# Expert stages of a four-layer attention and mixture-of-experts kernel: loops written out tile by tile, load order and the last bias changed

## What is computed

```
layer 0: 8 experts, best 2 a row, SwiGLU with 352 hidden units, and a shared expert
layer 1: 8 experts, best 1 a row, silu(x W1 + b1) W2 + b2 with 1,024 hidden units
layer 2: twice 32 experts, best 2 a row, SwiGLU with 128 hidden units, the two results averaged
layer 3: 32 experts, best 1 a row, SwiGLU, a fixed capacity of 80 rows an expert
y[row] = sum over the chosen experts e of weight(row, e) * expert_e(xn[row])
```

## Time and profile before

| | |
|---|---|
| runs | 2778.6 us in the median of three (2777.9 to 2780.2) |
| the profiled execution's own time | 2782.8 us |
| its span, first to last instruction | 2781.0 us |
| TensorE, products | busy 2143.0 us, 77% of the span |
| TensorE, weight loads | 1770.9 us, 64% |
| VectorE | 1327.0 us, 48% |
| ScalarE | 800.3 us, 29% |
| GpSimd | 790.9 us, 28% |
| mean granted TensorE clock | 0.868 of full speed |
| mean DMA rate | 124 GB/s over the span |

### The profile page before, as it was taken

The page is one execution under the profiler, slowest core; times in us unless marked ns, Lnnn a source line. Parts: engine busy times, 40 slices in busy tenths (PEclk is TensorE's granted clock), DMA queues, the critical chain, the costliest instruction groups (busy, mean ns, idle before and its releaser), DMA issues. The chain is left out here.

```text
span 2781.0 us, 46883 instructions
## 1 busy us (share of the span) xinstructions
PE 2143.0 (77%) x14782; PEld 1770.9 (64%) x14782; DVE 1327.0 (48%) x3863; ACT 800.3 (29%) x1862; POOL 790.9 (28%) x1177
## 2 busy tenths in 40 slices
PE   6769889955999999985996599847705773687695
PEld 5656659945999899975885366546604662354584
DVE  3555422235788788853002577452235225575513
ACT  4603312222333333342233144512201222244211
POOL 1000012232444444430112122024452434231133
PEclk9869999977999999996998699759856995898687
DMA  2030019933111111005883344038823873442195
GB/s 72 23 110 8 0 61 363 319 99 89 39 39 39 40 39 35 19 7 193 297 302 131 110 135 127 13 118 267 238 72 106 271 227 95 118 120 57 60 317 174
DMA packets 158190, 344.26 MB, mean 124 GB/s; under 512 B 22608, under 2 KB 101968, under 8 KB 149712
## 3 DMA queue, kind: packets, MB, share of 16 engines
q1 hardware_dynamic: 141136, 296.08, 32.5%
q0 software_dynamic: 16896, 46.16, 6.3%
HBM read 282.52 MB, written 57.15 MB: 122 GB/s over the span
## 5 line engine op out<-in xcount | busy, mean ns | idle before, releaser
L1821 PEld LDWEIGHTS heads_ps_c<-heads_band,heads_sT 128*128 128x128 f32 x3072 | 362.0, 192 | 21.3 <-issue 17.4
L1821 PE MATMUL heads_ps_c<-heads_band,heads_sT 128*128 128x129 f32 x3072 | 367.4, 276 | 7.4 <-DVE heads_band L2039 7.2
L930 DVE COPY experts_y<-experts_ps_y 128x256 f32<-128x256 f32 (+1 forms) x224 | 94.9, 424 | 503.2 <-DMA y_rows<-experts_y 288.1
L1977 POOL TENSOR_SCALAR heads_band<-heads_shifts,heads_taps 128x130 f32<-128x130 f32 x384 | 253.7, 675 | 268.2 <-PE heads_ps_c L1821 264.5
L853 PE MATMUL experts_ps_y<-experts_w,experts_h 128*128 128x256 f32 (+2 forms) x1008 | 269.7, 396 | 73.9 <-DVE experts_h L922 73.8
L843 PE MATMUL experts_ps_g<-experts_xT,experts_w 128*128 128x128 f32 (+2 forms) x2016 | 278.4, 286 | 6.5 <-ACT experts_xT L885 4.4
L843 PEld LDWEIGHTS experts_ps_g<-experts_xT,experts_w 128*128 128x128 f32 (+1 forms) x2016 | 258.1, 199 | 17.7 <-ACT experts_xT L885 12.2
L822 POOL DMA_INDIRECT experts_xg<-xn_rows,experts_x_ix x224 | 219.0, 978 | 176.4 <-POOL experts_x_ix L818 156.7
L818 POOL COPY experts_x_ix<-token_of 128x1 uint32 x224 | 41.5, 185 | 736.5 <-PEq L828 438.2
L853 PEld LDWEIGHTS experts_ps_y<-experts_w,experts_h 128*128 128x128 f32 (+2 forms) x1008 | 171.9, 189 | 113.2 <-DVE experts_h L922 93.7
L2039 DVE SCALAR_TENSOR_TENSOR heads_band<-heads_shifts,heads_taps,heads_band 128x130 f32<-128x130 f32 x768 | 226.3, 350 | 32.0 <-POOL heads_band L1977 27.5
(11 more groups left out here) (366 smaller groups left out, 3609.5 us busy)
## 6 DMA issues: line engine op xcount, KB each, us to landing
experts_w<-in_experts_dram SPq DMA_DIRECT2D x24, 2180.0 KB, 9.4
experts_w<-in_experts_dram SPq DMA_DIRECT2D x128, 384.0 KB, 4.6
experts_w<-in_experts_dram SPq DMA_DIRECT2D x40, 1088.0 KB, 8.6
y_rows<-experts_y SPq DMA_DIRECT2D x192, 128.0 KB, 8.9
experts_w<-in_experts_dram SPq DMA_DIRECT2D x32, 768.0 KB, 7.0
piece_rows<-heads_pieces SPq DMA_DIRECT2D x96, 192.0 KB, 2.6
heads_stackQ<-piece_rows SPq DMA_DIRECT2D x48, 192.0 KB
heads_stackK<-piece_rows SPq DMA_DIRECT2D x48, 192.0 KB
```

The costliest lines, as they stand in the source:

```text
L930: v.tensor_copy(y[0:rows, u % 2, :], ps_y[0:rows, u % 2, 0:D]).then_inc(y_copied, 1)
L1821: last = pe.matmul(out[:, qc * SEQ + k0:qc * SEQ + k1], sT[:, h % 2, kc, qc * P + dq:qc * P + dq + P], band[:, h % 2, dq, w0:w0 + k1 - k0] ...
L1977: last = pool.tensor_scalar(band[:, h % 2, dq, :], shifts[:, 0, :], taps[:, r % 2, h, dq * TAPS:dq * TAPS + 1], None, ALU.mult)
```

## The change

1. In `experts_stage` every engine's loop over blocks is written out over all tiles, so that the stagger of TensorE's three parts runs through the whole stage. All addresses are constants.
2. GpSimd hands column j of `token_of` to the gather directly, without the copy, and waits on `turned` (the transposition of tile j - ahead) rather than `y_ready`.
3. SyncE's load j waits on `y_copied` (the copy of tile j - ahead) rather than `y_ready`. The order of its queue stays: load j, store j - ahead.
4. NT is one less in layer 0 (39) and layer 1 (23), which still suffices: 8 experts can't leave more than 7 tiles over.
5. In experts1 the product with b2 goes; b2 is stored in all 128 rows of the weights, and VectorE adds it in the pass that took the output out of PSUM.
6. Waits that were made by giving semaphores a start value are made with `if j >= 2`.

```diff
 def experts_stage(...)
-        x_ix = s.sb("x_ix", [P, ahead, 1], U32)
-        b2 = lambda p: w[0:1, p, down_at + NF * D + NF:down_at + NF * D + NF + D]
+        b2 = lambda p: w[0:rows, p, down_at + NF * D + NF:down_at + NF * D + NF + D]
...
         def _(pool):
-            with pool.Fori(0, NT // ahead) as i:
-                for u in range(ahead):
-                    j = ahead * i + u
-
-                    pool.wait_ge(y_ready, j + 1)
-                    pool.tensor_copy(x_ix[:, u, :], tb.token_of[:, bass.ds(j, 1)]).then_inc(ix_ready, 1)
-                    pool.wait_ge(ix_ready, j + 1)
-
-                    pool.sem_inc(ix_passed, 1)
-                    pool.indirect_dma_start(xg[:, u, :], None, xn_dram,
-                                            bass.IndirectOffsetOnAxis(ap=x_ix[:, u, :], axis=0))\
-                        .then_inc(x_in[u], 16)
+            for j in range(NT):
+                if j >= ahead:
+                    pool.wait_ge(turned, j - ahead + 1)
+                pool.indirect_dma_start(xg[:, j % ahead, :], None, xn_dram,
+                                        bass.IndirectOffsetOnAxis(ap=tb.token_of[:, j:j + 1], axis=0))\
+                    .then_inc(x_in[j % ahead], 16)
...
         def _(pe):
-            def turn_rows(i, u):
-                pe.wait_ge(x_in[u], 16 * (i + 1))
+            def turn_rows(j):
+                pe.wait_ge(x_in[j % ahead], 16 * (j // ahead + 1))
+                if j >= 2:
+                    pe.wait_ge(xT_ready, j - 1)
...
+            def hidden_layer(j):
+                pe.wait_ge(xT_ready, j + 1)
+                pe.wait_ge(w_in[u], 16 * (j // ahead + 1))
+                if j >= 2:
+                    pe.wait_ge(h_ready, j - 1)
...
-                if biased:
-                    last = pe.matmul(ps_y[0:rows, p, 0:D], ones[0:1, 0:rows], b2(u), start=False, stop=True)
...
-            with pe.Fori(0, NT // ahead) as i:
-                for step in range(ahead + 2):
-                    for lag, part in enumerate((turn_rows, hidden_layer, output_layer)):
-                        if 0 <= step - lag < ahead:
-                            part(i, step - lag)
+            for step in range(NT + 2):
+                for lag, part in enumerate((turn_rows, hidden_layer, output_layer)):
+                    if 0 <= step - lag < NT:
+                        part(step - lag)
...
         def _(act):
-            with act.Fori(0, NT // ahead) as i:
-                for step in range(ahead + 1):
+            for step in range(NT + 1):
+                if step < NT:
+                    copy_rows(step)
+                if step >= 1:
+                    nonlinear(step - 1)
...
         def _(v):
-            def copy_out(i, u):
-                v.wait_ge(y_ready, ahead * i + u + 1 + ahead)
-
-                v.wait_ge(stored[u % 2], 16 * (ahead // 2 * i + u // 2 + 1))
-                v.tensor_copy(y[0:rows, u % 2, :], ps_y[0:rows, u % 2, 0:D]).then_inc(y_copied, 1)
+            def copy_out(j):
+                p = j % 2
+                v.wait_ge(y_ready, j + 1)
+                if j >= 2:
+                    v.wait_ge(stored[p], 16 * (j // 2))
+                if biased:
+                    v.tensor_tensor(y[0:rows, p, :], ps_y[0:rows, p, 0:D], b2(j % ahead), ALU.add)\
+                        .then_inc(y_copied, 1)
+                else:
+                    v.tensor_copy(y[0:rows, p, :], ps_y[0:rows, p, 0:D]).then_inc(y_copied, 1)
...
         def _(sp):
-            def load_weights(i, u):
-                j = ahead * i + u
-
-                sp.wait_ge(y_ready, j + 1)
-
-                sp.sem_inc(w_passed, 1)
-                row = sp.value_load(tb.weights_of[0:1, bass.ds(j, 1)], min_val=0, max_val=w_dram.shape[0] - P)
-                sp.dma_start(w[:, u, :], w_dram[bass.ds(row, P), :]).then_inc(w_in[u], 16)
+            def load_weights(j):
+                u = j % ahead
+                if j >= ahead:
+                    sp.wait_ge(y_copied, j - ahead + 1)
+                row = sp.value_load(tb.weights_of[0:1, j:j + 1], min_val=0, max_val=w_dram.shape[0] - P)
+                sp.dma_start(w[:, u, :], w_dram[bass.ds(row, P), :]).then_inc(w_in[u], 16)
+
+            def store(j):
+                sp.wait_ge(y_copied, j + 1)
+                sp.dma_start(y_dram[j * rows:(j + 1) * rows, :], y[0:rows, j % 2, :]).then_inc(stored[j % 2], 16)
+
+            for j in range(NT + ahead):
+                if j < NT:
+                    load_weights(j)
+                if j >= ahead:
+                    store(j - ahead)
...
 def build(...)
-        NT = TILES * 2 + 8
+        NT = TILES * 2 + 7
...
-        NT = TILES + 8
+        NT = TILES + 7
```

More of the change, by code:

```diff
@@ L842, in hidden_layer @@
                         for c in range(DC):
[L843 removed]
+                            last = pe.matmul(ps[0:m, p, f * P:f * P + rows], wt[:, c, f * P:f * P + m],
                                              xT[:, p, c, 0:rows], start=(c == 0), stop=(c == DC - 1))
                 last.then_inc(gu_ready, 1)
[L847 to L857 removed]
@@ L859, in _, with output_layer @@
-            with pe.Fori(0, NT // ahead) as i:
-                for step in range(ahead + 2):
-                    for lag, part in enumerate((turn_rows, hidden_layer, output_layer)):
-                        if 0 <= step - lag < ahead:
-                            part(i, step - lag)
+            def output_layer(j):
+                p, u = j % 2, j % ahead
+                pe.wait_ge(h_ready, j + 1)
+                if j >= 2:
+                    pe.wait_ge(y_copied, j - 1)
+                for f, m in enumerate(chunks):
+                    last = pe.matmul(ps_y[0:rows, p, 0:D], h[0:m, p, f, :], down_w(u)[0:m, f, :],
+                                     start=(f == 0), stop=(f == NF - 1))
+                last.then_inc(y_ready, 1)
@@ L924, in multiply @@
                 last.then_inc(h_ready, 1)
-            def copy_out(i, u):
-                v.wait_ge(y_ready, ahead * i + u + 1 + ahead)
-                v.wait_ge(stored[u % 2], 16 * (ahead // 2 * i + u // 2 + 1))
-                v.tensor_copy(y[0:rows, u % 2, :], ps_y[0:rows, u % 2, 0:D]).then_inc(y_copied, 1)
-            with v.Fori(0, NT // ahead) as i:
-                for step in range(ahead + 1):
-                    if step < ahead and not biased:
-                        multiply(i, step)
-                    if step >= 1:
-                        copy_out(i, step - 1)
+            def copy_out(j):
+                p = j % 2
+                v.wait_ge(y_ready, j + 1)
+                if j >= 2:
+                    v.wait_ge(stored[p], 16 * (j // 2))
+                if biased:
+                    v.tensor_tensor(y[0:rows, p, :], ps_y[0:rows, p, 0:D], b2(j % ahead), ALU.add)\
+                        .then_inc(y_copied, 1)
+                else:
+                    v.tensor_copy(y[0:rows, p, :], ps_y[0:rows, p, 0:D]).then_inc(y_copied, 1)
@@ L939, in _ @@
+            for step in range(NT + 1):
+                if step < NT and not biased:
+                    multiply(step)
+                if step >= 1:
+                    copy_out(step - 1)
         @block.sync
         def _(sp):
-            for p in range(2):
-                sp.sem_inc(stored[p], 16)
-            def load_weights(i, u):
-                j = ahead * i + u
-                sp.wait_ge(y_ready, j + 1)
-                sp.sem_inc(w_passed, 1)
-                row = sp.value_load(tb.weights_of[0:1, bass.ds(j, 1)], min_val=0, max_val=w_dram.shape[0] - P)
-                sp.dma_start(w[:, u, :], w_dram[bass.ds(row, P), :]).then_inc(w_in[u], 16)
@@ L953, in store @@
-            def store(i, u):
-                j = ahead * i + u
-                sp.wait_ge(y_copied, j + 3)
-                sp.dma_start(y_dram[dyn(j, rows), :], y[0:rows, u % 2, :]).then_inc(stored[u % 2], 16)
-            for u in range(ahead):
-                load_weights(0, u)
-            with sp.Fori(1, NT // ahead) as i:
-                for u in range(ahead):
-                    load_weights(i, u)
-                    store(i - 1, u)
-            for u in range(ahead):
-                store(NT // ahead - 1, u)
```

59 lines of the change are left out of this document (20 added, 39 removed).

## The result

The changed kernel took **2793.7 us** in the median of 16 runs against 2780.6 us for the kernel before in the same comparison: a ratio of 1.0048, 95% interval 1.0035 to 1.0060, so 13 us slower, and the whole interval lies on the slow side. The forecast was 2789, slower.

The account below looks back on a forecast made before the run. Experts2 and experts3 were taken as paced by a two-tile loop of copy, store and landing. Terms -1 (experts0), -28 (experts1), +28 (experts2), +12 (experts3) gave +11 us on 2782.8, so 2789 in the median, range 2757 to 2824.

Parts of the forecast that it names:

- rival 1: The forecast itself: the store loop, lengthened by the load in front, outweighs experts1's gain; 2785 to 2815 us, chance 0.45.
- SyncE's offsets: In experts2 the load leaves 1.23 us and the store 1.64 us after the start of the copy.
- The pace of experts2: 2.85 us a tile for 2.586 and 2.525, costing 12.7 and 15.6 us in the two experts2 stages.
- the shift of the twelve block starts: Twelve eight-tile block starts in experts2, each shifted to a load at 1.23 us, gave a mean of 2.85 us a tile.
- Rival 2: Queue empties, loads land in shortest times: 2.44 us a tile in experts2, sum -43, about 2736 us; chance 0.22.
- The start of experts2: Directly read index columns take 3.3 us off each stage (bounds 0 and 4.68), cancelling 3.3 us added for the backlog.
- Experts0: Pace of 4.45 us a tile, one tile less included: -1 us (-6 at 4.18, +14 at 5.1).
- Experts3: Pace of 3.7 us a tile for 3.172, over 22 tiles: +12 us.
- Experts1: Bias on VectorE, no gather wait or drain, one tile less: step of 7.4 us, stage -28 us.
- Rival 3: The two halves cancel to within 5.6 us, needing a pace near 2.73 us; chance 0.20.
- Rival 4: Queue stays as full as now: 3.09 us a tile in experts2, 4.19 in experts3, +50, so 2829 us; chance 0.07.
- Rival 5: The loops' 26 back jumps each cost an instruction fetch of 1.0 us; ending them gives 2763 us; chance 0.06.

Follow-up runs that it names:

- u_gather_old: Changed kernel with the gathers as before: index column copied by GpSimd, a wait for that copy, release by y_ready instead of turned; 2816.4 us, ratio 1.0094.
- u_y4: Changed kernel with four y buffers in SBUF rather than two, nothing else; 2672.1 us, ratio 0.9614.
- u_bias_pe: Changed kernel with the last bias of experts1 back on TensorE (product of ones with b2), plain copy on VectorE; 2824.9 us, ratio 1.0130.
- u_nt_old: Changed kernel with 40 tiles again in layer 0 and 24 in layer 1; 2805.7 us, ratio 1.0079.
- b_y4: Kernel before the change, loops kept, with four y buffers instead of two, nothing else; 2744.0 us, ratio 0.9837.
- u_load_early: Changed kernel with weight loads waiting on y_ready again, not on the copy, in every expert stage but experts1; 2723.2 us, ratio 0.9791.
- u_y8: Changed kernel with eight y buffers, order of load and store as changed; 2657.7 us, ratio 0.9558.

## Why the prediction was right, and where it was not

Sign, size and range held, by the mechanism of rival 1: the load in front of the store lengthens the loop over two tiles. That the sum came within 2 us is luck: experts0 was missed by 11 us, and experts1 and the two experts2 stages together by 4.5 and 6.5 the other way.

*SyncE's offsets.* Forecast 1.23 and 1.64 us after the copy, measured 1.19 and 1.57.

*The pace of experts2.* Forecast 2.85 us, measured 2.76 and 2.77. The step that failed is the shift of the twelve block starts: they were taken just after a backlog of stores, and the new loop has none; that this is why they came out too long was not tested. Nor were all twelve what the text says: in three of them the load had left 0.12, 0.42 and 1.10 us before the copy. By the form itself, half of 1.57 + 3.93 (from the issue of the store to the next copy but one, mean) is 2.75; the 3.93 are 3.84 of landing and 0.09 until VectorE starts. The waits of VectorE for stores grew by 41.7 us over both stages, from 83.2 and 83.7 to 104.7 and 103.9, for the 30 forecast. Rival 2 wanted landings of 3.2 us; with a quieter queue, a DMA share of 0.82, the median is 3.7 and 3.8, and single loads get down to 3.1. Its own turning point was a landing of 3.7, a pace of 2.68. The median is there, but the mean is 3.84, and the pace goes by the mean. The Trainium skill ("DMA: Bandwidth & Descriptors", section Anatomy of one DMA) fits a DMA that GpSimd issues with about 2.0 us plus bytes / 436 GB/s, an estimated 3.2 us for the 512 KB of load and store together. These DMAs are SyncE's, and the medians here are 0.5 us and more above that.

*The start of experts2.* I had set a loss of 3.3 us by the drained backlog against a gain of 3.3 by earlier gathers. The second turn waited 3.79 us after 4.68:

```profile
1841.85 0.69 PE L824 MATMUL experts_ps_x<-ident,experts_xg 128*128 128x128 f32 x2 [3.79 <-DMA experts_xg<-xn_rows,token_of]
```

From the first gather to the ninth copy the stages take 37.0 and 34.9 us where they took 35.1 and 33.2, so +1.9 and +1.8, and u_gather_old puts the share of the index copies and the release at -0.2 and +1.4 us. The lower bound, 0, was nearer than the upper. What cancels this is the tail: from copy 56 to the last 1.1 and 0.6 us less. The middle gives 48 x (2.757 - 2.586) = +8.2 and 48 x (2.766 - 2.525) = +11.6.

*Experts0* is the term I mis-sized most: -1 for +10.0. Two parts of it. The pace: I took 4.45, between 4.18 and 5.1, in the belief that an emptier queue would shorten the landing; it hardly did. The loads take 8.0 us (5.4 to 9.2) where they took 8.5, and the copies come in unequal pairs:

```profile
532.46 0.42 DVE L923 COPY experts_y<-experts_ps_y 128x256 f32<-128x256 f32 x1 [6.28 <-DMA y_rows<-experts_y]
535.68 0.42 DVE L923 COPY experts_y<-experts_ps_y 128x256 f32<-128x256 f32 x1 [2.27 <-DMA y_rows<-experts_y]
543.08 0.42 DVE L923 COPY experts_y<-experts_ps_y 128x256 f32<-128x256 f32 x1 [6.45 <-DMA y_rows<-experts_y]
```

That is 10.62 us for two tiles here, 2 x 4.77 in the mean. 23 tiles at 4.77 instead of 4.45 are +7.4 us. And the start, which I had not priced: from the first gather to the ninth copy 60.5 us for 52.4, so +8.0; the third copy came 14.0 us after the second (9.4 before), for it waits for store 0, which is issued behind load 8 and the first backlog and lands 16.6 us later. The end gave 4.6 us back (22.0 for the 26.6 I had summed), and -1 + 7.4 + 8.0 - 4.6 is +9.8. (My low value for this stage, -6 at 4.18 us a tile, should have been -7; it is used in rival 2 alone.) u_y4, without that loop, has experts0 at 173.8 us, and TensorE's own 4.18 us a tile.

*Experts3*: +13.8 for +12, but by two errors that offset each other. The pace from the third copy to copy 24 is 3.58 us, not 3.7 (22 x 0.41 = +9), and the stage's start, again not priced, is 5.3 us longer. In the other kernels with the changed queue order (u_bias_pe, u_gather_old, u_nt_old) the stage took 123 to 126 us, so its +13.8 carries some 4 us of chance.

*Experts1*: -32.5 for -28. The step is 7.26 us for 7.4, the mis-sized term being the bias, 0.76 for 0.65 us. The gather's wait was smaller in the kernel before than the 0.41 us of u_gather_old: there, with the loops drained in each block, a gather was issued 7.8 to 18.9 us ahead of its turn (I had said two steps), and TensorE's waits in the 16 tiles of the earlier trace rows are these:

```profile
PE experts_ps_x L833 <- DMA experts_xg<-xn_rows,experts_x_ix: 1.7, 2, 1.4
PE experts_ps_g L843 <- ACT experts_xT L885: 1.0, 4, 0.2
```

So of 8.34 us a tile the bias is 0.76 and the gather's wait 0.11, and 0.21 is left above the 7.26 of the changed kernel. Of that, 0.06 is the second row, one wait in each block of four tiles; the rest has no row of its own. It goes by what is left to the drain between blocks, which no run tested alone. Over 23 tiles the 1.08 us make 24.8, and the tile less adds 7 to 8 (u_nt_old: 7.0). A load must land within two steps less 1.3 us. At 7.26 us a step that is 13.2 to 13.3 us, not 13.5; the loads took 10.9 us in the median and 13.3 at most. The longest landed at 1370.6 us, just as the hidden layer that reads it was due. TensorE never waited, but this stage has nothing in hand.

*The rivals.* Rival 3 (2773 to 2784) and rival 2 are out by the paces. Rival 4 is out in experts2 (3.09 us) and experts3 (4.19 us); only experts0 was as slow as it had it, 4.77 us for 4.7. Rival 5, the back jumps: the written-out kernel fetched 120 packets of instructions instead of 89, the stages' gains and losses are explained without it, and no wait of TensorE shows a stall it would have ended. On SyncE the jump does cost, some 0.65 us a pass in b_y4 (2.6 for 1.97 us a pair); the trace does not say whether that is a fetch or the instructions around the branch. What I missed about the loops is this cost to SyncE, with that of computed addresses: it did not matter with two buffers and the load released late, but u_load_early, with the same release of the loads as the kernel before, is 53 us faster than it (2723.2 for 2776.4 beside it), 32.6 of them in experts1 and 18.4 in the two experts2 stages, where the store leaves 0.46 us after the copy rather than 0.80.

## What to carry to other kernels

When a double-buffered output paces a stage, write its loop out as a sum (copy to issue, issue to landing, landing to copy, over the number of buffers), and look at what stands in front of the store in its queue: an edit that only moves a load from before the copy to behind it cost 70 us of 2,720. Price the start of each stage apart from its steady pace, for the first stores wait behind the whole backlog of first loads. And before tuning the order of a queue, add buffers: four for two gave 0.9614 here, and store first with them 0.9568 (the intervals just overlap), where order alone gave 0.9751. Last, writing a loop out moves the points at which its buffers come free: the old release of the gather cost 0.11 us a tile in the loops and 0.41 written out.

## What I had not expected of the hardware

- In experts2 a 128 KB store takes as long to land as the 384 KB load issued 0.38 us ahead of it, 3.8 and 3.7 us in the median. Issued ahead of its tile's load it took 4.1 us, but with the DMA engines busier (share 0.91 for 0.82), so the order alone is not priced by this.
- 1,088 KB loads took 8.0 us with the DMA engines busy for 0.86 of the time and 8.5 us with 0.93: a lighter load on the queue did not shorten them.
- The DMA engines were full (share 1.01) at 324 to 327 GB/s in experts2 with more `y` buffers, but moved 413 GB/s in experts0's backlog. More than half of the difference goes by the gathers. Packets, MB and share of the engines' time in the same window of u_y8, of the loads and stores (q1) and of the gathers (q0):

```profile
q1 hardware_dynamic: 14135, 25.72, 73.3%
q0 software_dynamic: 2302, 6.28, 27.8%
```

  A fifth of the bytes takes more than a quarter of the time; from 1893 to 1930 us it is 37.8% for 1.84 of 9.35 MB. Why the gathers are slower late in the stage was not tried.
- A load and a store at computed addresses cost SyncE 1.97 us in the median without any waiting, and 2.6 us across the loop's back jump (b_y4); with constant addresses (u_y4) two loads, with the store between, are issued 1.6 us apart.
